# Row-by-row gates and a three-buffer mix in the last node phase of a four-layer graph network

## What is computed

```python
deg = segment_sum(ones, dst); nsum = segment_sum(feat[src], dst)
h_neigh = where(deg > 0, nsum / maximum(deg, 1), 0)
fs = feat @ w_self + b_self;  fn = h_neigh @ w_neigh + b_neigh
low, high = relu(fs + fn), relu(fs - fn)
identity = relu(feat @ w_id + b_id)
def _att(x, a, b):
    norm = linalg.norm(x, axis=1) + 1e-16
    return sigmoid(elu5(x / norm @ a + b))        # elu5: x > 0 ? x : 5 * expm1(x)
out = 3 * (att_low * low + att_high * high + att_mlp * identity)
x = layernorm(x + out)
```

## Time and profile before

| | |
|---|---|
| median of three runs | 4543.78 us (4543.26, 4543.78, 4559.67) |
| profiled execution | 4544.45 us, its span 4542.7 us |
| busy: PE, DVE, ACT, POOL | 2958.0, 2460.2, 976.3, 3225.0 us |
| mean granted PE clock | 0.743 |

### The profile page before, as it was taken

The page is one execution under the profiler, slowest core; times in us unless marked ns, Lnnn a source line. Parts: engine busy times, 40 slices in busy tenths (PEclk is TensorE's granted clock), DMA queues, the critical chain, the costliest instruction groups (busy, mean ns, idle before and its releaser), DMA issues.

```text
span 4542.7 us, 56741 instructions
## 1 busy us (share of the span) xinstructions
PE 2958.0 (65%) x17142; PEld 2462.2 (54%) x17142; DVE 2460.2 (54%) x5101; ACT 976.3 (21%) x2136; POOL 3225.0 (71%) x3338
## 2 busy tenths in 40 slices
PE   4555555556887888884488888888735554445554
PEld 3444444445776777774377777777634443334443
DVE  7655555655666666664655555555572323323348
ACT  0100000013333333331222222222241111111125
POOL 7777777757777777775777777777627777777751
PEclk8555555558999999997699999999965555555566
DMA  4252222225777777773366666666422221121221
GB/s 109 55 170 53 53 53 53 53 66 149 196 195 193 197 196 192 199 195 90 96 170 155 159 155 155 159 155 158 107 66 53 52 53 52 52 53 52 53 60 52
DMA packets 600630, 514.44 MB, mean 113 GB/s; under 512 B 99790, under 2 KB 532093, under 8 KB 600334
## 3 DMA queue, kind: packets, MB, share of 16 engines
q0 software_dynamic: 105472, 216.60, 19.1%
q10 hardware_dynamic: 210704, 154.61, 12.6%
q1 hardware_dynamic: 284158, 139.62, 11.4%
HBM read 410.93 MB, written 91.26 MB: 111 GB/s over the span
## 4 chain that ended last, share of the span: by engine, by line
POOL 51%; issue 18%; DVE 4%; PE 2%; DMA 1%; DVEq 1%; ACT 1%; POOLq 0%; ACTq 0%
POOL g L547 24%; POOL nodes L547 16%; POOL work L547 8%; PE bank L647 2%; POOL acc L583 1%; POOL xr_by_rank L593 1%; POOL b_by_rank L593 1%; DMA nodes<-a_src,srct 1%; DVE bst L1419 1%; DMA g<-a_src,srct 0%; DVE work L1893 0%; DVE z_mix L1887 0%; PE bank L652 0%; DVE z_mix L1882 0%; DVEq L1881 0%
## 5 line engine op out<-in xcount | busy, mean ns | idle before, releaser
L1372 DVE TENSOR_TENSOR acc<-bank,acc 128x512 f32 x588 | 407.0, 692 | 1081.2 <-PE bank L647 1008.4
L647 PEld LDWEIGHTS bank<-quads,work 128*128 128x128 f32 x3920 | 593.0, 226 | 326.7 <-issue 317.8
L647 PE MATMUL bank<-quads,work 128*128 128x128 f32 x3920 | 632.8, 315 | 198.7 <-DMA work<-x,srct 197.3
L647 PE MATMUL bank<-quads,g 128*128 128x128 f32 x1568 | 391.6, 429 | 533.8 <-DMA g<-x,srct 326.1
L990 ACT COPY bank<-zeros 128x384 f32<-128x384 f32 x588 | 283.3, 482 | 1732.5 <-DVE acc L1372 1690.3
L647 PEld LDWEIGHTS bank<-quads,g 128*128 128x128 f32 x1568 | 340.2, 320 | 581.3 <-issue 559.1
L547 POOL DMA_INDIRECT g<-x,srct x392 | 379.3, 968 | 172.9 <-issue 119.2
L547 POOL DMA_INDIRECT g<-xl,srct x392 | 378.6, 966 | 119.5 <-issue 119.5
L547 POOL DMA_INDIRECT g<-a_src,srct x392 | 378.6, 966 | 119.5 <-issue 117.3
L547 POOL DMA_INDIRECT nodes<-a_src,srct x390 | 376.2, 965 | 118.9 <-issue 116.4
L547 POOL DMA_INDIRECT nodes<-xl,srct x390 | 375.6, 963 | 118.9 <-issue 118.9
(11 more groups left out here) (329 smaller groups left out, 5528.9 us busy)
## 6 DMA issues: line engine op xcount, KB each, us to landing
partial<-acc ACTq DMA_DIRECT2D x196, 288.0 KB, 3.1
work<-local_rank ACTq DMA_DIRECT2D x392, 128.0 KB
work<-xr_by_rank SPq DMA_DIRECT2D x784, 64.0 KB
work<-b_by_rank SPq DMA_DIRECT2D x784, 64.0 KB
work<-in_rel_t ACTq DMA_DIRECT2D x196, 128.0 KB
g<-acc SPq DMA_DIRECT2D x126, 64.0 KB
g<-in_x,srct POOLq DMA_INDIRECT x392
scan_penalties<-work SPq DMA_DIRECT2D x14, 448.0 KB
```

What stands on the lines that cost most here:

```text
L647: return nc.tensor.matmul(to, lhsT, rhs, start=start, stop=stop, skip_group_check=True)
L1372: v.tensor_tensor(window, partial_bank(l, q)[:, :], window, ALU.add).then_inc(partial_copied, 1)
```

## The change

In the last node phase DVE applies the gates by rows: seven `scalar_tensor_tensor` of 128x128 add low times its gate to the state, seven add high times its gate, seven `bn_stats` follow, for batch b-1, in small groups between the steps of batch b's gate chain. `mix` has three buffers, the sums alternate between two, the statistics too. Waits on semaphores take the place of drains, the chain is algebraically shortened from 14 to 11 small operations on DVE, and ACT runs a batch further ahead. The steps beside the last sweep begin one quad earlier, and its own gate is applied by seven row operations. In the sweeps a number of waits are moved into a matmul group, placed less often or dropped; POOL waits every fourth quad; DVE's drains before `accumulate` go; the two one-hot operations of the node count become one; and SP's window addresses come from a table of byte offsets, which takes its rows from 3576 to 538.

```diff
+        mixes = (mix, *(rows_14.rearrange("p (b k) f -> p b (k f)", k=2) for rows_14 in (nodes[:, 2 * BT:, :], g[:, 2 * BT:, :])))
+        sums_y = (y7, nt7)
-         STEP_ROOT, STEP_SCORE, STEP_EXP, STEP_ELU, STEP_EXP2, STEP_MIX) = range(1, 29, 2)
+         STEP_ROOT, STEP_SCORE, STEP_EXP, STEP_ELU, STEP_EXP2, STEP_MIX) = range(0, 28, 2)
...
-                    if i >= RING and i % 2 == 0:
-                        pool.wait_ge(rows_used, before + i + 2 - RING)
+                    if i % GATHER_QUADS == 0 and i + GATHER_QUADS > RING:
+                        pool.wait_ge(rows_used, before + i + GATHER_QUADS - RING)
...
                     for t in range(TQ):
+                        if t == TQ - 1 and l == 3 and i + 1 < NQ:
+                            pe.wait_ge(gathered[(i + 1) % RING], quad_gathered(l, i + 1))
                         last = mm(to[:, bass.ds(off[t], P) if t else slice(0, P)], ...
...
+            copy_rows_2(0)
+            mix_rows(0)
+            copy_rows_2(1)
+            squares(0)
+            for b in range(NBAT):
+                if b + 1 < NBAT:
+                    mix_rows(b + 1)
+                if b + 2 < NBAT:
+                    copy_rows_2(b + 2)
+                gates(b)
+                if b >= 1:
+                    root(4 * NBAT + b - 1, (b - 1) % 2)
+                if b + 1 < NBAT:
+                    squares(b + 1)
+                if b >= 2:
+                    results(b - 2)
+            root(4 * NBAT + NBAT - 1, (NBAT - 1) % 2)
+            results(NBAT - 2)
             results(NBAT - 1)
...
+                    if k < BT:
+                        last = v.scalar_tensor_tensor(out=y, in0=mixes[b % 3][:, r, 0:D], scalar=gate_of[:, b % 2, 2 * r:2 * r + 1],
+                                                      in1=xa[:, b * BT + r, :], op0=ALU.mult, op1=ALU.add)
+                    elif k < 2 * BT:
+                        last = v.scalar_tensor_tensor(out=y, in0=mixes[b % 3][:, r, D:], scalar=gate_of[:, b % 2, 2 * r + 1:2 * r + 2],
+                                                      in1=y, op0=ALU.mult, op1=ALU.add)
+                    else:
+                        last = v.bn_stats(bst[:, r, :], y)
...
+                of_row(0, 2)
+                root_inverse(z_mix, u)
+                of_row(2, 4)
+                root_corrected(z_mix, u)
...
+                of_row(13, 16)
+                elu_shifted(z_mix, u)
+                of_row(16, 19)
+                third_of_sum(z_mix, u)
+                of_row(19, 21)
+                gate_found(gate_of[:, b % 2, :], z_mix, u)
+                if before >= 0:
+                    variances(before)
```

More of the change, by code:

```diff
@@ L1233, in squares @@
             def squares(b):
[L1234 to L1235 removed]
+                act.wait_ge(mix_copied, b + 2)
+                nc.scalar.activation(mix_sq[:], mixes[b % 3], ACT.Square).then_inc(square_ready, 1)
             def gates(b):
@@ new lines, in own_gate @@
+                    gate_found(z_id[:, 3, :], z_id, b)
+                    dve.wait_ge(gates_done, b + 1)
+                    for r in range(BT):
+                        last = v.scalar_tensor_tensor(out=xa[:, b * BT + r, :], in0=y7[:, r, :], scalar=z_id[:, 3, r:r + 1],
+                                                      in1=xa[:, b * BT + r, :], op0=ALU.mult, op1=ALU.add)
+                    last.then_inc(mix_read, 1)
+                if is_batch(b, NBAT - 1) and q == STEP_MIX:
+                    last_blocks[:] = loaded_values(mybir.EngineType.DVE, block_rank, 0, BT, NPAD)
@@ L1895, in gates @@
-                dve.drain()
-                dve.sem_inc(mix_read, 1)
-                v.tensor_tensor(nt7[:], mix_a[:, :, 0:D], mix_a[:, :, D:], ALU.add)
-                dve.drain()
-                if b >= 1:
-                    dve.wait_ge(out_ready, b)
-                v.tensor_tensor(y7[:], nt7[:], states(b), ALU.add)
-                dve.drain()
-                norm_stats(y7)
-            first_windows(2)
-            dots(0)
-            gates(0)
-            for b in range(1, NBAT):
-                dots(b)
-                norm_shift(4 * NBAT + b - 1)
-                gates(b)
@@ new lines, in rows @@
+            def rows(b, first, end):
+                for k in range(first, end):
+                    r, y = k % BT, sums_y[b % 2][:, k % BT, :]
+                    if k == 0:
+                        if b >= 2:
+                            dve.wait_ge(out_ready, b - 1)
+                        dve.wait_ge(gates_done, NBAT + b + 1)
+                    if k == BT:
+                        dve.wait_ge(row_step, 3 * b + 1)
+                    if k == 2 * BT:
+                        dve.wait_ge(mix_read, NBAT + b + 2)
+                    if k < BT:
+                        last = v.scalar_tensor_tensor(out=y, in0=mixes[b % 3][:, r, 0:D], scalar=gate_of[:, b % 2, 2 * r:2 * r + 1],
+                                                      in1=xa[:, b * BT + r, :], op0=ALU.mult, op1=ALU.add)
+                    elif k < 2 * BT:
[3 more added lines that the diff above has]
+                        last = v.bn_stats(bst[:, r, :], y)
+                    if k in (BT - 1, 3 * BT - 1):
+                        last.then_inc(row_step, 1)
+                    if k == 2 * BT - 1:
+                        last.then_inc(mix_read, 1)
@@ L1916 @@
+            shift_found(NBAT - 1)
 def kernel(**inputs):
```

320 lines of the change are left out of this document (203 added, 117 removed).

## The result

| | before | changed kernel |
|---|---|---|
| median of 7 executions | 4543.78 us | 4531.36 us |
| lowest and highest | 4541.52, 4559.67 | 4522.46, 4533.70 |
| profiled execution, its span | 4544.45, 4542.7 | 4532.43, 4530.6 |
| last node phase (last gather to the end) | 176.1 | 162.5 |
| dots to dots where nothing disturbs | 18.36 | 13.44 |

The ratio is 0.9963, 95% interval 0.9953 to 0.9972: 17 us faster by the ratio of the executions, 12 by the medians, and either way less than the 0.5% that the prediction took as its threshold. The forecast was 4536, 4.6 us too high; the time lies in its range of 4519 to 4547, and no measurable change was its likeliest case. The parts of the sum hold less well than the sum, and on one of the chips of the study the change was 8.5% slower, a size that none of its parts foresaw.

What follows compares the result with a forecast made beforehand. POOL's gathers bound the sweeps; in the last node phase ACT's list and R would bind, about 16 us a batch. Span 4535.7 - 1 = 4534.7, plus 1.75 around it 4536.5, allowing for the median 4536; range 4519 to 4547.

Steps and rivals of the forecast that it cites:

- no measurable change: Whole kernel: time differs by no more than 0.5%, 22.7 us, from before; chance 0.79.
- the sixth variance: Last node phase: the variance of the sixth batch comes at 4516.4, after summed batch periods and 4 us for POOL.
- The sweeps: Four sweeps: POOL's gather issue covers the edits, so 0, bounds -4 and +5; 1 us saved on own-gate passes.
- Rival 5: Sweeps: POOL is held 1 us at each fourth quad of one sweep, +49, giving 4585 us; chance 0.02.
- Price of a row: Last node phase, DVE: one gated 128x128 row operation takes 0.24 us, between 0.21 and 0.27.
- Ten chain operations: Last node phase, DVE: the gate chain's ten small operations between rows take some 0.15 us each, 1.5 together.
- R: Last node phase: time from a batch's root operation on DVE to the variance of the batch in front, 7.0 us.
- Rival 2: Last node phase: interleaving works fully, rows 0.21, no collision, DVE never idle, dots 14.6 us apart; 4521 us; chance 0.23.
- DVE 7.7 and ACT 9.3 to the next root operation: Last node phase: from variance to next root operation DVE needs 7.7 us, ACT 9.3, so ACT is later; period 16.3.
- the mark: Last node phase: DVE idle 1 to 2 us ahead of the chain's first reciprocal, released by ACT, would show the forecast right.
- Collisions: Last node phase: DVE stands still while POOL multiplies `sel`; three left, charged 2.0, 0.5 and 1.5 us.
- The fill: Start of the last node phase: ACT's order delays batch 0's gates; first reciprocal near 4414, first variance 4435.7.

Runs made afterwards that it cites:

- the hand-made lag: Changed kernel with PE, in the fourth sweep, holding a quad's last matmul until gathers ten quads further on land: 4696.54 us against 4556.51 before, ratio 1.0306.
- two quads: Changed kernel with POOL waiting for ring space at every second quad instead of every fourth: 4527.94 us, ratio 0.9959 to the kernel before.
- the gates first: Changed kernel with ACT answering the gate chains of batches 0 and 1 before the next mix and windows: 4531.82 us, ratio 0.9959 to the kernel before.
- in place: Changed kernel with gated sums and normalised results written over the batch's own states: 4529.18 us, ratio 0.9959 to the kernel before.

## Why the prediction was right, step by step

The total came out 4.6 us too high. That it came so near is luck in part, since it is the balance of larger misses: the sum ran 7.5 us late up to the sixth variance and was 2.4 us short behind it.

- **The sweeps, 0 with -1 for contention: right** on the first chip (every one within 1.5 us, together 1.4 us shorter), and on the others like it within what the chips differ by. The 2.4 us by which the first gather starts later were in no term. The reason, that room for ten quads is above the lag, was an argument from one chip; on another the lag is 55 us and more, and the reason falls. Rival 5 had the mechanism and the place, and its price per wait is the one that the hand-made lag showed: 3.2 us at 45 waits, 141 in the sweep. It counted 49 waits to a sweep; there are 46.
- **Price of a row, 0.24 between 0.21 and 0.27: too low.** 14 rows take 3.85 us when nothing stands between them, 0.275 each. The Trainium skill (VectorE: DVE Perf Modes, section on the TRN2 errata) gives N+151 cycles for an fp32 `tensor_tensor`, by which the prediction estimated 0.29 for a row; the measurement is nearer to that than to the middle it took, and just over its upper bound of 0.27.
- **Ten chain operations at 0.15: too high.** The 6.3 us from root operation to variance hold twelve rows (3.3), seven statistics (1.5) and 0.7 for aggregation and variance; 0.8 is left for ten operations, 0.08 each. With rows between them they cost their start-to-start time and nothing of their latency. R was 7.0 in the sum and is 6.3. Rival 2 had 5.9: its chain steps "all but free" were right, its rows at 0.21 were not.
- **DVE 7.7 and ACT 9.3 to the next root operation: 7.15 and 8.7.** That ACT binds was half right. "DVE idle 1 to 2 us ahead of the chain's first reciprocal" was the mark that the prediction gave for it, and in this trace it isn't there: where ACT was late, DVE was as late with a stalled product. The mark did show in the runs with two quads, with the gates first and in place, at 15.06. Collisions were charged at 2.0, 0.5 and 1.5; they cost 1.9, 0.2 and 0.8 (15.3 and 15.9 less those 15.06). Periods 15.3 and not 16.3, 13.4 and not 14.7.
- **The fill: right.** First reciprocal of batch 0 near 4414: 4415.54, in a phase that began 1.5 us later. First variance 4435.7: 4435.40.
- **The sixth variance: 4516.4 in the sum, 4508.9 measured.** This is the term that was mis-sized, by 7.5 us: R gives 3.5 of it (five times 0.7), the way from the variance to the next root operation 2.9 (five times some 0.6), collisions 1.1.
- **The end: the store's wait (3.4, measured 3.08) was in the sum; the 2.49 us of DVE for ACT's results of batch 4 were not.** The prediction followed each wait on the output buffer and not the one on the sums, which alternate between two.
- **The start, 1.3 us earlier: 0.9** by the clock and 2.4 after the last gather, of which the fill keeps 0.9.
- **Not told apart in the sum:** the same chain, shorter and without drains, is worth 0.85 us a batch even without interleaving. The prediction hid it under the rows.

The chances: "no measurable change" at 0.79 was what happened. Between the mechanisms the run decides less kindly. The first reciprocal and the sweeps came as the forecast said. But the loop ran at 14.7 us on average (five intervals, 73.35 us) with DVE never idle for ACT's root in them, and that is the sign that the prediction had given for rival 2, under "wrong". Neither stands whole: rival 2 wanted no collisions and rows at 0.21, and there were three collisions and rows at 0.275; the forecast wanted ACT to bind alone, and DVE was as late.

## What to carry to other kernels

Moving work into another batch's latency pays in the loop and is paid back at the ends: the loop gained 21 us here and the tail returned nearly 9, of which 2.5 and 3.1 are waits on buffers for which nobody waited so long while the loop was slower. Before changing how often a producer asks for room, measure the lag of its consumer and keep a margin for a chip on which it is longer, since a lag that reaches the room costs at every wait. When data seem late, look first whether the transfer or the engine that takes it is late. And undo the parts one at a time: a cheap part of this change, the shorter chain without drains, gave 6.4 of the phase's 13.6 us by itself.

## What was not expected of the hardware

The same kernel took 4531 us on one chip and 6202 on another, with engine instructions of the same length and gathers that landed as soon (1.26 us after their issue): PE, DVE and ACT paused there for 15 to 43 us some twenty times in a sweep of 1121 us. What makes them pause, no run shows. Among chips of the faster kind the second sweep was 991 to 998 us. TensorE's granted clock over the same stretch of PE's list was 1.00 in one execution and 0.88 in another, of a kernel with the same list on PE, with 12.0 and 13.7 us a batch. And a DVE product of 128x7 values that takes 0.16 us took up to 2.05 beside POOL's multiply of the selection, ending 0.02 us after it. The Trainium skill (SBUF — State Buffer, section "Who interferes with whom") has the rule: a DVE instruction with two SBUF inputs and a POOL instruction that reads SBUF contend, and the later one fully blocks. The trace agrees; whether one is hit is decided by where it stands, and in the run with two quads one batch was missed and took 15.06 us where the changed kernel's took 15.9.
